# ScalarE is told of a finished score product by the product that follows it

## The reference

```python
Q = _split_heads(x @ Wq.T + bq)
K = _split_heads(x @ Wk.T + bk)
V = _split_heads(x @ Wv.T + bv)
cQ = Q + tQ          # tQ, tK: the same projections of the condition's token
cK = K + tK
scores = jnp.einsum('bhqd,bhkd->bhqk', cQ, cK) / jnp.sqrt(jnp.float32(HEAD_DIM))
attn = jax.nn.softmax(scores, axis=-1)
out = jnp.einsum('bhqk,bhkd->bhqd', attn, V)
x = x + out.transpose(0, 2, 1, 3).reshape(B, S, D_MODEL)
```

## Time and profile before

| | |
|---|---|
| time, median of 3 runs | 656.06 us (655.94 to 656.4) |
| span of the profiled execution | 654.2 us |
| the profiled execution's own time | not given apart from its span; the median stands 1.9 us above the span |
| PE busy | 647.3 us, 99% of the span |
| PEld, DVE, ACT, POOL busy | 68%, 83%, 60%, 74% |
| granted TensorE clock | nine tenths or more in all 40 slices (1.00 in the stretches asked for) |

### The profile page before, as it was taken

The page is one execution under the profiler, slowest core; times in us unless marked ns, Lnnn a source line. Parts: engine busy times, 40 slices in busy tenths (PEclk is TensorE's granted clock), DMA queues, the critical chain, the costliest instruction groups (busy, mean ns, idle before and its releaser), DMA issues.

```text
span 654.2 us, 10054 instructions
## 1 busy us (share of the span) xinstructions
PE 647.3 (99%) x3528; PEld 442.8 (68%) x3528; DVE 540.6 (83%) x815; ACT 389.6 (60%) x684; POOL 487.4 (74%) x204
## 2 busy tenths in 40 slices
PE   9999999999999999999999999999999999999997
PEld 6776677666677666676666776666776666776542
DVE  5776888888888888888888888888888888888787
ACT  6455666565566565666556665556665555564773
POOL 6338877778877779777779777779777788666992
PEclk9999999999999999999999999999999999999999
DMA  8944333555333555333554434553434544424501
GB/s 260 255 97 115 103 107 87 143 147 140 97 110 94 144 147 132 97 108 103 146 146 125 104 96 114 146 147 107 116 90 127 146 131 124 119 67 110 151 18 65
DMA packets 48038, 79.87 MB, mean 122 GB/s; under 512 B 9458, under 2 KB 9714, under 8 KB 47986
## 3 DMA queue, kind: packets, MB, share of 16 engines
q1 hardware_dynamic: 47632, 79.07, 45.1%
q10 hardware_dynamic: 356, 0.16, 0.1%
HBM read 19.95 MB, written 8.39 MB: 43 GB/s over the span
## 4 chain that ended last, share of the span: by engine, by line
PE 95%; DVE 2%; issue 1%; ACT 1%; DMA 1%; ACTq 0%; POOLq 0%; DVEq 0%
PE bank L350 27%; PE bank L442 18%; PE bank L420 18%; PE bank L462 16%; PE bank L398 14%; DVE bank L737 1%; PE bank L368 1%; ACT Pt L637 1%; DMA Qs<-mt 1%; DVE part_sums L762 0%; DVE rr L786 0%; DVE ends L807 0%; PE bank L470 0%; DVE rr L775 0%; DVE bank L793 0%
## 5 line engine op out<-in xcount | busy, mean ns | idle before, releaser
L637 ACT ACTIVATE Pt<-bank 128x512 f32<-128x512 f32 x512 | 299.2, 600 | 216.3 <-PE bank L442 144.8
L737 DVE TENSOR_REDUCE mf<-bank 128x1 f32<-128x512 f32 x496 | 332.6, 686 | 72.3 <-PE bank L420 69.3
L943 POOL TENSOR_TENSOR A<-A,Pt 128x2048 f32<-128x2048 f32 x59 | 270.9, 4592 | 4.6
L442 PE MATMUL bank<-Qs,Ks 98*128 98x512 f32 x496 | 197.5, 404 | 1.4 <-DMA Qs<-mt 1.4
L420 PE MATMUL bank<-Ks,Qs 96*128 96x512 f32 x496 | 197.6, 399 | 0.2
L943 POOL TENSOR_TENSOR A<-Pt 128x2048 f32<-128x2048 f32 x30 | 138.4, 4614 | 9.3 <-DVE part_sums L762 9.3
L442 PEld LDWEIGHTS bank<-Qs,Ks 98*128 98x128 f32 x496 | 93.1, 188 | 52.1 <-ACT Pt L637 25.9
L462 PE MATMUL bank<-Pt,V 128*32 128x512 f32 x1024 | 118.9, 596 | 0.0
L913 POOL TENSOR_TENSOR Xl<-xr,Xh 128x512 fp32r<-128x512 f32 x28 | 36.1, 1291 | 110.0 <-ACT Xh L598 110.0
L420 PEld LDWEIGHTS bank<-Ks,Qs 96*128 96x128 f32 x496 | 93.8, 189 | 26.7 <-DVE bank L737 3.0
L350 PE MATMUL bank<-Xh,Wl 128*128 128x512 f32 x256 | 102.2, 399 | 0.0
(11 more groups left out here) (73 smaller groups left out, 389.4 us busy)
## 6 DMA issues: line engine op xcount, KB each, us to landing
Qs<-hi SPq DMA_DIRECT2D x60, 256.0 KB, 3.6
Ks<-hi SPq DMA_DIRECT2D x60, 256.0 KB, 3.6
Qs<-lo SPq DMA_DIRECT2D x30, 256.0 KB, 4.1
Ks<-lo SPq DMA_DIRECT2D x30, 256.0 KB, 3.4
xr<-xT SPq DMA_DIRECT2D x28, 256.0 KB, 2.7
res<-xT SPq DMA_DIRECT2D x28, 256.0 KB, 2.9
outT<-ot SPq DMA_DIRECT2D x28, 256.0 KB, 3.1
Qs<-mt SPq DMA_DIRECT2D x122, 4.0 KB
```

Source lines behind the costliest of these rows:

```text
L442: e.matmul(st_bank(u)[:, :], k[0:98, j, kc * P:(kc + 1) * P], q[0:98, j, :], start=True, stop=True).then_inc(t_st, 1)
L637: e.activation(exponentials(g)[:, kc, j, :], st_bank(u)[:, :], ACT.Exp, scale=SCALE).then_inc(a_e, 1)
L737: e.reduce_max(to[:, 4 * j + qc:4 * j + qc + 1], MXB[u % 2][:, :], AXX).then_inc(v_mx, 1)
L943: e.tensor_tensor(sums, ex[:, 0, :, :] if kc == 1 else sums, ex[:, kc, :, :], ALU.add).then_inc(p_a, 1)
```

## The change

The order of instructions on each engine stays as it was, one by one. Where a product for maxima stands right behind a score product in its slot, the score product no longer increments `t_st`, and whoever waited for that score waits for the increment of `t_mx` by the product for maxima behind it. Where none stands there (slot 0 of round 0, some slots of rounds 25 to 30, all of round 31) `t_st` stays and counts those alone. The tables have 15 slots with a product for maxima in round 0, 24 x 16 in rounds 1 to 24, and 66 in rounds 25 to 30: 465 of 512 increments go, 47 stay.

```diff
+        told_by, plain, u = [], 0, OPENING
+        for t in range(G):
+            for n in range(SLOTS):
+                if maxima_at(t, n):
+                    told_by.append((t_mx, u + 1))
+                    u += maxima_at(t, n)
+                else:
+                    plain += 1
+                    told_by.append((t_st, plain))
+
+        def scored(u):
+            return told_by[u]
...
-                e.matmul(st_bank(u)[:, :], k[0:98, j, kc * P:(kc + 1) * P], q[0:98, j, :],
-                         start=True, stop=True).then_inc(t_st, 1)
+                m = e.matmul(st_bank(u)[:, :], k[0:98, j, kc * P:(kc + 1) * P], q[0:98, j, :],
+                             start=True, stop=True)
+                if not maxima_at(g, n):
+                    m.then_inc(t_st, 1)
...
-                e.wait_ge(t_st, u + 1)
+                e.wait_ge(*scored(u))
                 e.activation(exponentials(g)[:, kc, j, :], st_bank(u)[:, :], ACT.Exp, scale=SCALE).then_inc(a_e, 1)
...
-                    e.wait_ge(t_st, SLOTS * (stack_before(g) + 1))
+                    e.wait_ge(*scored(SLOTS * (stack_before(g) + 1) - 1))
```

## The result

| | before | after |
|---|---|---|
| median of 7 runs each | 656.08 us (655.94 to 656.40) | 658.47 us (656.70 to 658.89) |
| ratio after / before | | 1.0027, 95% interval 1.0017 to 1.0038 |
| span of the profiled execution | 654.2 us | 654.9 us (that run took 656.7 us, the fastest of the seven) |

What follows compares the result with a forecast made beforehand. TensorE, busy for 99% of the span, was taken as the bound. Increments 0, rounds 1 to 24 +1.0 and rounds 25 to 30 +0.8 gave +1.8 us on 656.06, so 657.9 us (+0.28%), range 656.1 to 659.3.

Steps and rivals of the forecast that it cites:

- case D: Whole kernel: the forecast itself, 657.9 us, own range 656.9 to 659.2, chance 0.62.
- Increments at 0: TensorE: removing 465 increments saves no time; taken as 0, bounds 0 to 1 us.
- Rival A: TensorE: an increment does take time, so the change is faster, 651.4 us without stalls or 653.2 with; chance 0.08.
- Slots with room: Five-product slots: 1.07 us left hides the 0.234 us delay entirely; slot 12 just fits with 0.28 us less 0.05.
- about 70 more: Score products (t,15) and (t+1,1): about 70 more weight-load waits for ScalarE, some 0.05 us after an exponential's end.
- SyncE: SyncE's copies of a group used much later: 0.234 us later costs nothing, since 11.6 us of cover remain.
- Two links of 0.02 us a round, 1.0 us: Rounds 1 to 24, chain of slots 13, 15, 1: two links lose 0.02 us each, 0.04 us a round.
- the chain 14, 0: Three-product slots: runs beside chain 13, 15, 1, covered by the shift slot 15 already brought, so adds no loss.
- Rival B: Rounds 1 to 24: late loads stay hidden, only the last rounds pay 0.4 us; 656.5 us, chance 0.22.
- Rival C: Three-product slots: lateness shows whole, two links at 0.15 us in 24 rounds; 664.5 us, chance 0.08.
- The last rounds, 0.8 us: Rounds 25 to 30: five places without margin lose 0.10 to 0.23 us, mean 0.15; bounds 0.3 to 1.5 us.
- The four other places: Besides score product (25,15): one place in round 27, three in 29 and 30, 0.10 to 0.23 us each.

Runs made afterwards that it cites:

- experiment 3: Kernel before the change, with 1056 projection products that had no increment now incrementing a semaphore nobody reads: 656.02 us, ratio 0.9997.
- experiment 2: Changed kernel with its later waits, but the 465 score products still increment a semaphore, one nobody reads: 659.05 us, ratio 1.0046.
- experiment 4: Kernel before, with the change in slots 2 to 11 of rounds 1 to 24 alone, 240 increments removed: 656.31 us, ratio 1.0001.
- Experiment 6: Changed kernel, but score products 13 and 15 of rounds 1 to 24 keep their own increments: 658.48 us, ratio 1.0037.
- experiment 5: Changed kernel, but score product 14 of rounds 1 to 24 keeps its own increment: 657.39 us, ratio 1.0019.
- experiment 7: Kernel before, with the change in rounds 25 to 30 alone: 656.78 us, ratio 1.0009.
- experiment 8: Changed kernel, with TensorE's wait for the rows of maxima moved behind the previous round's slot 15 score product, in rounds 2 to 25: 657.68 us, ratio 1.0021.

## Why the prediction came out as it did

**The direction and the sum.** Forecast +1.8 us, measured +2.4 us between the medians; the time lies within the range and within case D. By terms it was 0, +1.9 and +0.6 where the prediction had 0, +1.0 and +0.8. The mechanism held (later exponentials make weight loads late in the slots with three products, and nothing else costs): exponentials start 0.27 us after the score product's end, slots of five products still last 1.17 us. That the sum came so near is in part luck, since the second term was half of what it should be and the third a little too large.

**Increments at 0.** Right, and now shown rather than read off distances: at most 0.4 ns each (experiment 3), and no difference in rounds 1 to 24 with or without them (experiment 2). Rival A is out.

**Slots with room.** Right for slots 2 to 11 (experiment 4). In slot 12, which experiment 4 leaves out, the 0.28 us just sufficed as forecast, in all rounds but 14: there the load of slot 14 had no room at all. The earlier trace rows show slots 13 and 15 of that round; its slot 12 wasn't read. It cost some 0.15 us, once, which the prediction's 24 equal rounds didn't have.

**The waits of the earlier trace rows.** Misread. I wrote that most of the 39 are in rounds 25 to 31; 23 are in rounds 1 to 24, in slot 2, and the exponential named had ended 1.90 us earlier. The sum doesn't use them, but the forecast of about 70 more does, and it was wrong by half.

**SyncE.** Its wait moved to the product for maxima and is longer, 27.5 us against 20.6; experiment 4 does not test it, since slot 15 keeps its increment there. What can be said is that in none of the nine profiles did a product or a weight load wait for a copy of the projections' queries or keys.

**Two links of 0.02 us a round, 1.0 us.** The mechanism was right and the term mis-sized: a round lost 0.080 us in the mean (0.073 without round 14), 1.9 us in all. The step that failed is "the chain 14, 0 runs beside it and is covered by the shift that slot 15 already brought". I took the response of 0.05 us from slot 15 of round 25 for all slots. The score product of slot 0 waits for two semaphores, the rows of maxima and the bank, and its load answers 0.11 us after the exponential; the trace before the change shows it once, where the load of (29,0) starts at 610.13, 0.11 us after the end of exponential (28,14). Room there was for 0.13 us only (exponential 14 of round 16 ends at 371.57, the load of slot 0 is at 371.70). With that response, read after the result, the prediction's own rule gives the right size: before the change an exponential ends 0.40 + 0.04 + 0.60 = 1.04 us after its score product's start; in slots of three products the load two slots on is due 6 x 0.234 - 0.234 = 1.17 us after that start; of the 0.13 us between them 0.11 are needed; so the load is 0.234 - 0.02 = 0.21 us late, 0.12 are hidden and 0.09 lost. Experiment 6 measured 0.085, or 0.079 without round 14. Without slot 14 the other chain costs 0.037, or 0.031, for which the prediction had 0.04 (experiment 5). That fits the 0.12 us of hidden lateness and the 0.05 us of response; neither was varied by itself.

**Rival B** (all hidden in rounds 1 to 24) is out: the rounds are longer in every profile that has the later exponentials in slots 13 to 15, and experiment 5 still loses 0.89 us with the worst link gone. **Rival C** (the lateness shows whole) is out too: it wanted 0.3 us a round.

**The last rounds, 0.8 us.** 0.5 to 0.6 us (experiment 7, the traces), within its bounds, but as a difference of two things. Score product (31,1), before and after:

```profile
633.14 0.39 PE L442 MATMUL bank<-Qs,Ks 98*128 98x512 f32 x1
634.11 0.40 PE L455 MATMUL bank<-Qs,Ks 98*128 98x512 f32 x1
```

From the first score product of round 25 to here it is 103.21 us before and 104.11 after: rounds 25 to 30 lose 0.9 us, 0.1 more than forecast. From here to the end of the span it is 21.1 and 20.8 us: the end gives 0.3 us back. The prediction had nothing given back there. The place worked out, score product (25,15), reads after the change:

```profile
548.30 1.09 ACT L652 ACTIVATE Pt<-bank 128x512 f32<-128x512 f32 x2 [0.48 <-PE bank L433]
548.58 0.39 PE L411 MATMUL bank<-Wvh,Xh 128*128 128x512 f32 x1
548.95 0.19 PEld L455 LDWEIGHTS bank<-Qs,Ks 98*128 98x128 f32 x1 [0.42 <-ACT Pt L652]
548.95 0.50 PE L455 MATMUL bank<-Qs,Ks 98*128 98x512 f32 x1
549.29 0.40 PE L433 MATMUL bank<-Ks,Qs 96*128 96x512 f32 x1
549.53 0.40 PE L411 MATMUL bank<-Wvh,Xl 128*128 128x512 f32 x1
```

The score product ends 549.45 - 548.58 = 0.87 us after the start of the product before it, against 549.12 - 548.48 = 0.64 in the earlier trace rows: 0.23 lost, and the product for maxima behind it is back to 0.40 us, so that the projection after it starts 0.95 us after the one ahead of the score instead of 0.80: 0.15 net, for which the prediction had 0.14. The four other places were counted and not worked out. By the starts of the rounds, round 25 is 0.19 us longer than before, round 27 0.07, round 29 0.46 and round 30 0.20, rounds 26 and 28 not at all: the losses are in the rounds that were named.

## What to carry to other kernels

An increment on TensorE's product is worth nothing that could be measured here; when it comes is worth 2.4 us. Before a wait is moved to a later instruction, go round the loop (product, exponential, the product that reuses the bank) for each slot length apart, with the response that belongs to the waiting instruction's number of semaphores, and take the longest chain and not the sum of the links. And a loss here shows neither in the busy share nor in the whole span of one profile: compare the starts of the same instruction, round against round. A wait that the profile puts down to an engine is one only if that engine ended just before: look up its end.

## What the runs showed that was not expected

- A weight load that waits for two semaphores, of which ScalarE's comes last, started 0.11 us after the exponential's end, one that waits for ScalarE's alone 0.05 us (experiment 8, and the profile after).
- In round 14 one exponential starts 0.28 us later than its like in the other rounds, in every profile and at the same place; the cause is open.
- The wait for the first rows of maxima, 1.4 us, was there in six of the eight kernels profiled in the experiments and in the kernel before, and not in the other two nor in the kernel after. The first score product starts anywhere from 37.9 to 40.9 us in the ten profiles, and the wait is part of that.
